# A carry scan over chunk ends: nine narrow steps in place of seven wide ones

## The reference, cut to what matters

```python
x = x + layernorm(attn(layernorm(x)))       # x: 8 x 1024 x 512
x = x + layernorm(ffn(layernorm(x)))

def attn(x):
    s = sigmoid(silu(x @ s_w1.T + s_b1) @ s_w2.T + s_b2)
    u = (x @ B_w.T + B_b) * s                # 8 x 1024 x 128
    h[t] = h[t - 1] @ A.T + u[t]             # the recurrence over 1024 tokens, h[-1] = 0
    y = h @ C_w.T + C_b + x @ D_w.T + D_b
    return y * sigmoid(x @ g_w.T + g_b)

def ffn(x):
    out_shared = relu(x @ Ws1) ** 2 @ Ws2
    # and a sum over routed experts, weighted by trunc(softmax of the two best)
    return out_shared + out_routed
```

## Time and profile before

| | us |
|---|---|
| median of 3 runs | 800.49 (800.29 to 800.89) |
| profiled execution, its own time | 800.6 |
| span of that execution (first to last instruction) | 798.6 |
| PE busy | 783.3 (98%) |
| PEld busy (beside PE) | 648.0 (81%) |
| DVE busy | 605.9 (76%) |
| POOL busy | 456.4 (57%) |
| ACT busy | 344.4 (43%) |

### The profile page before, as it was taken

The page is one execution under the profiler, slowest core; times in us unless marked ns, Lnnn a source line. Parts: engine busy times, 40 slices in busy tenths (PEclk is TensorE's granted clock), DMA queues, the critical chain, the costliest instruction groups (busy, mean ns, idle before and its releaser), DMA issues. The chain is left out here.

```text
span 798.6 us, 10778 instructions
## 1 busy us (share of the span) xinstructions
PE 783.3 (98%) x3628; PEld 648.0 (81%) x3628; DVE 605.9 (76%) x1404; ACT 344.4 (43%) x554; POOL 456.4 (57%) x553
## 2 busy tenths in 40 slices
PE   7999999999999999999999999999999999999996
PEld 6878888888888888888888888888888888888875
DVE  7868896598956897678975889649896589734895
ACT  4535354344434554245443535435443444432353
POOL 1253658548465576466674665845757557644445
PEclk9999999999999999999999999999999999999999
DMA  8534434454355425552345533454425442232222
GB/s 269 207 107 158 137 94 138 160 184 134 87 177 174 161 89 158 183 187 80 95 143 185 185 101 96 147 185 168 149 80 182 150 143 80 78 133 87 65 113 106
DMA packets 40767, 110.90 MB, mean 139 GB/s; under 512 B 7044, under 2 KB 24836, under 8 KB 32903
## 3 DMA queue, kind: packets, MB, share of 16 engines
q1 hardware_dynamic: 40278, 110.00, 41.4%
q10 hardware_dynamic: 432, 0.20, 0.1%
HBM read 60.84 MB, written 33.61 MB: 118 GB/s over the span
## 5 line engine op out<-in xcount | busy, mean ns | idle before, releaser
L499 PE MATMUL TM<-gw_hi,xT_hi 128*128 128x512 f32 x256 | 107.3, 419 | 0.0
L1982 POOL TENSOR_TENSOR xres<-work,xres 128x512 f32<-128x512 f32 x56 | 75.1, 1341 | 52.8 <-DVE work L1332 52.8
L501 PE MATMUL TM<-gw_hi,xT_lo 128*128 128x512 f32 x256 | 100.6, 393 | 0.0
L501 PE MATMUL TM<-dw_hi,xT_lo 128*128 128x512 f32 x256 | 100.2, 391 | 0.0
L500 PE MATMUL TM<-gw_lo,xT_hi 128*128 128x512 f32 x256 | 100.0, 391 | 0.0
L499 PE MATMUL TM<-dw_hi,xT_hi 128*128 128x512 f32 x256 | 99.9, 390 | 0.0
L500 PE MATMUL TM<-dw_lo,xT_hi 128*128 128x512 f32 x256 | 99.6, 389 | 0.0
L996 ACT ACTIVATE work<-TM,nmz,rsz 128x512 f32<-128x512 f32 x62 | 48.2, 777 | 106.7 <-POOL nmz L1952 106.7
L1942 POOL TENSOR_TENSOR rsv<-rsv,negh 128x1 f32<-128x1 f32 x64 | 47.1, 736 | 82.3 <-DVE rsv L1328 82.2
L1997 POOL TENSOR_TENSOR x2T_lo<-work,x2T_hi 128x512 fp32r<-128x512 f32 x60 | 78.5, 1319 | 2.0 <-ACT x2T_hi L926 1.9
L1990 POOL TENSOR_TENSOR work<-work,xres 128x512 f32<-128x512 f32 x60 | 76.7, 1295 | 1.3 <-ACT work L996 1.3
(11 more groups left out here) (189 smaller groups left out, 2063.1 us busy)
## 6 DMA issues: line engine op xcount, KB each, us to landing
xres<-in_x SPq DMA_DIRECT2D x16, 1024.0 KB, 5.9
x_scratch<-xres SPq DMA_DIRECT2D x16, 1024.0 KB, 4.7
xin<-in_x SPq DMA_DIRECT2D x15, 1024.0 KB, 5.3
work<-x2q SPq DMA_DIRECT2D x120, 128.0 KB, 2.7
out<-work SPq DMA_DIRECT2D x30, 512.0 KB, 3.2
xin<-in_x_t SPq DMA_DIRECT2D x14, 1024.0 KB, 6.2
rows_in<-ln_scratch SPq DMA_DIRECT2D x14, 512.0 KB, 4.7
xin<-in_x SPq DMA_DIRECT2D x2, 512.0 KB, 5.0
```

The costliest lines, as they stand in the source:

```text
L499: eng.matmul(ps, lhs[0], rhs[0], start=first, stop=False)
L501: return eng.matmul(ps, lhs[1], rhs[0], start=False, stop=last)
L1982: eng.tensor_tensor(xres[:, j, :], work[:, j, :], xres[:, j, :], ALU.add).then_inc(S["x1_ok"], 1)
```

## The change

Nine steps carry over the chunk ends in place of seven. The odd columns are added to the even ones (pairs), every second pair to the next (pairs of pairs), five doubling steps run over every fourth column, and two steps go down again, to the columns 6, 10, .. and then to the odd ones. They read and write `carry` at strides of 2 and 4 columns. The slices sum to 64 + 32 + 31 + 30 + 28 + 24 + 16 + 31 + 63 = 319 columns. The inner steps become 10 to 16, so a scan has 17 steps. The lists of PE, ACT, DVE and POOL in the tails are written anew.

```diff
--- before.py
+++ after.py
...
@@ -218,6 +218,10 @@
                 POWERS.append((at[3 * k], plain, at[2 * k]))
             k, plain = 2 * k, twice
 
+        CARRY_STEPS = [(slice(1, 128, 2), slice(2, 129, 2), L), (slice(2, 127, 4), slice(4, 129, 4), 2 * L)]
+        CARRY_STEPS += [(slice(4, 129 - 4 * s, 4), slice(4 + 4 * s, 129, 4), 4 * L * s) for s in (1, 2, 4, 8, 16)]
+        CARRY_STEPS += [(slice(4, 125, 4), slice(6, 127, 4), 2 * L), (slice(2, 127, 2), slice(3, 128, 2), L)]
+
         def power_of(i):
             return (SC, *TR)[i % 3][:, 0:P]
 
@@ -534,11 +538,12 @@
                     for j in range(L - 1):
                         m = eng.matmul(SC[:, 0:P], apt[:, idx[L - 1 - j], :], u[:, j, :],
                                        start=(j == 0), stop=(j == L - 2))
-                elif i <= 7:
-                    s = 2 ** (i - 1)
-                    m = eng.matmul(SC[:, s:P], apt[:, idx[L * s], :], carry[:, 1:1 + P - s], start=True, stop=True)
+                elif i <= 9:
+                    src, dst, k = CARRY_STEPS[i - 1]
+                    n = (dst.stop - dst.start - 1) // dst.step + 1
+                    m = eng.matmul(SC[:, 0:n], apt[:, idx[k], :], carry[:, src], start=True, stop=True)
                 else:
-                    j = i - 8
+                    j = i - 10
                     prev = carry[:, 0:P] if j == 0 else u[:, j - 1, :]
                     m = eng.matmul(SC[:, 0:P], apt[:, 0, :], prev, start=True, stop=True)
                 m.then_inc(S["scan_done"], 1)
@@ -690,34 +695,32 @@
 
             def first_tail(b, rep):
                 a = (b, rep)
-                G(*a, 0, {0: 0, 2: 1})
-                scan_step(*a, 2)
-                G(*a, 1, {0: 3, 1: 4, 2: 5})
-                scan_step(*a, 6)
-                G(*a, 2, {0: 7, 1: 8, 2: 9})
-                scan_step(*a, 10)
+                G(*a, 0, {0: 0, 1: 1, 2: 2})
+                scan_step(*a, 3)
+                G(*a, 1, {0: 4, 1: 5, 2: 6})
+                scan_step(*a, 7)
+                G(*a, 2, {0: 8, 1: 9, 2: 10})
                 scan_step(*a, 11)
-                G(*a, 3, {1: 12})
-                scan_step(*a, 13)
-                scan_step(*a, 14)
+                G(*a, 3, {0: 12, 1: 13, 2: 14})
+                scan_step(*a, 15)
+                scan_step(*a, 16)
 
             def tail(b, rep):
                 a = (b, rep)
                 G(*a, 0, {0: 0, 1: 1, 2: 2})
-                W1f(*a, 1, 0)
-                scan_step(*a, 3)
-                W1f(*a, 1, 1, {0: 4})
-                G(*a, 1, {0: 5, 1: 6})
-                scan_step(*a, 7)
-                G(*a, 2, {1: 8, 2: 9})
-                scan_step(*a, 10)
+                W1f(*a, 1, 0, {1: 3})
+                scan_step(*a, 4)
+                W1f(*a, 1, 1, {0: 5, 2: 6})
+                G(*a, 1, {0: 7, 1: 8})
+                scan_step(*a, 9)
+                G(*a, 2, {0: 10, 1: 11, 2: 12})
                 W2(*a, 4)
-                scan_step(*a, 11)
+                scan_step(*a, 13)
                 W2(*a, 5)
-                scan_step(*a, 12)
-                G(*a, 3, {2: 13})
+                scan_step(*a, 14)
+                G(*a, 3, {1: 15})
                 W2(*a, 6)
-                scan_step(*a, 14)
+                scan_step(*a, 16)
                 W2(*a, 7)
 
             def body(b, rep):
@@ -757,14 +760,15 @@
                 scan_step(*a, 4)
                 W1f(*a, 1, 1, {0: 5, 1: 6})
                 scan_step(*a, 7)
-                G(*a, 1, {0: 8, 1: 9})
-                G(*a, 2, {1: 10, 2: 11})
+                G(*a, 1, {0: 8, 1: 9, 2: 10})
+                G(*a, 2, {0: 11, 1: 12})
+                scan_step(*a, 13)
                 W2(*a, 4)
                 W2(*a, 5)
-                G(*a, 3, {0: 12, 1: 13})
+                G(*a, 3, {0: 14, 1: 15})
                 W2(*a, 6)
+                scan_step(*a, 16)
                 W2(*a, 7)
-                scan_step(*a, 14)
 
             def last_body(b, rep):
                 a = (b, rep)
@@ -903,7 +907,7 @@
             def hs(b, rep, j):
 
                 if j < L - 1:
-                    eng.wait_ge(S["scan_ok"], body_at("scan_ok", b, 8 + j))
+                    eng.wait_ge(S["scan_ok"], body_at("scan_ok", b, 10 + j))
                 if j >= 2:
                     eng.wait_ge(S["y_done"], body_at("y_done", b, j - 2))
                 src = u[:, j, :] if j < L - 1 else carry[:, 1:P + 1]
@@ -999,9 +1003,9 @@
             def first_tail(b, rep):
                 a = (b, rep)
                 gate(*a, 0)
-                hs(*a, 0)
                 gate(*a, 1)
                 gate(*a, 2)
+                hs(*a, 0)
                 gate(*a, 3)
                 hs(*a, 1)
 
@@ -1009,13 +1013,13 @@
                 a = (b, rep)
                 hidden(*a, 1, 0)
                 hidden(*a, 1, 1)
-                hs(*a, 0)
                 gate(*a, 0)
                 gate(*a, 1)
+                hs(*a, 0)
+                hs(*a, 1)
                 gate(*a, 2)
                 zn(*a, 4)
                 zn(*a, 5)
-                hs(*a, 1)
                 gate(*a, 3)
                 zn(*a, 6)
                 zn(*a, 7)
@@ -1075,17 +1079,17 @@
 
             def last_tail(b, rep):
                 a = (b, rep)
+                gate(*a, 0)
                 hidden(*a, 1, 0)
-                gate(*a, 0)
+                gate(*a, 1)
                 hidden(*a, 1, 1)
-                gate(*a, 1)
+                hs(*a, 0)
                 gate(*a, 2)
-                hs(*a, 0)
                 zn(*a, 4)
                 zn(*a, 5)
                 gate(*a, 3)
+                hs(*a, 1)
                 zn(*a, 6)
-                hs(*a, 1)
                 zn(*a, 7)
 
             def last_body(b, rep):
@@ -1294,11 +1298,12 @@
                     if rep > 0:
                         eng.wait_ge(S["hs_hi_ok"], body_at("hs_hi_ok", b - 1, L - 1))
                     r = eng.tensor_tensor(carry[:, 1:P + 1], SC[:, 0:P], u[:, L - 1, :], ALU.add)
-                elif i <= 7:
-                    s = 2 ** (i - 1)
-                    r = eng.tensor_tensor(carry[:, 1 + s:P + 1], SC[:, s:P], carry[:, 1 + s:P + 1], ALU.add)
+                elif i <= 9:
+                    _, dst, _ = CARRY_STEPS[i - 1]
+                    n = (dst.stop - dst.start - 1) // dst.step + 1
+                    r = eng.tensor_tensor(carry[:, dst], SC[:, 0:n], carry[:, dst], ALU.add)
                 else:
-                    j = i - 8
+                    j = i - 10
                     r = eng.tensor_tensor(u[:, j, :], SC[:, 0:P], u[:, j, :], ALU.add)
                 r.then_inc(S["scan_ok"], 1)
 
@@ -1474,90 +1479,94 @@
                 scan_add(*a, 0)
                 l1_bn(b + 1, 0)
                 scan_add(*a, 1)
+                l1_bn(b + 1, 1)
                 scan_add(*a, 2)
-                l1_bn(b + 1, 1)
+                l1_bn(b + 1, 2)
                 scan_add(*a, 3)
-                l1_bn(b + 1, 2)
+                l1_ag(b + 1, 0)
                 scan_add(*a, 4)
-                l1_ag(b + 1, 0)
                 l1_ag(b + 1, 1)
-                l1_bn(b + 1, 3)
                 scan_add(*a, 5)
                 scan_add(*a, 6)
+                l1_ag(b + 1, 2)
                 scan_add(*a, 7)
+                l1_bn(b + 1, 3)
                 scan_add(*a, 8)
                 scan_add(*a, 9)
-                hs_low(*a, 0)
-                l1_ag(b + 1, 2)
+                l1_bn(b + 1, 4)
                 l1_ag(b + 1, 3)
+                l1_bn(b + 1, 5)
                 l1_ep(b + 1, 0)
                 scan_add(*a, 10)
-                l1_bn(b + 1, 4)
+                scan_add(*a, 11)
+                scan_add(*a, 12)
                 l1_ag(b + 1, 4)
-                scan_add(*a, 11)
-                l1_bn(b + 1, 5)
+                l1_ag(b + 1, 5)
                 l1_bn(b + 1, 6)
-                l1_ag(b + 1, 5)
+                scan_add(*a, 13)
+                l1_ag(b + 1, 6)
                 l1_bn(b + 1, 7)
-                l1_ag(b + 1, 6)
-                scan_add(*a, 12)
-                scan_add(*a, 13)
+                scan_add(*a, 14)
+                scan_add(*a, 15)
+                scan_add(*a, 16)
+                hs_low(*a, 0)
+                hs_low(*a, 1)
                 l1_ag(b + 1, 7)
                 l1_ep(b + 1, 1)
-                hs_low(*a, 1)
-                scan_add(*a, 14)
 
             def tail(b, rep):
                 a = (b, rep)
                 l1_bn(b + 1, 0)
+                l1_bn(b + 1, 1)
                 scan_add(*a, 0)
-                l1_bn(b + 1, 1)
+                l1_bn(b + 1, 2)
                 scan_add(*a, 1)
+                l1_bn(b + 1, 3)
+                l1_ag(b + 1, 0)
                 scan_add(*a, 2)
-                l1_bn(b + 1, 2)
-                l1_ag(b + 1, 0)
+                scan_add(*a, 3)
                 l1_ag(b + 1, 1)
-                l1_bn(b + 1, 3)
                 l1_bn(b + 1, 4)
-                l1_bn(b + 1, 5)
```

(64 more changed lines are left out.)

## The result

| | before | after |
|---|---|---|
| median of 6 runs each, us | 800.39 (800.18 to 800.89) | 803.76 (803.37 to 804.23) |
| profiled execution, its own time | 800.6 | 803.77 |
| its span | 798.6 | 801.7 |

The ratio is 1.0043, 95% interval [1.0032, 1.0053]: slower by 3.4 us. The forecast was 804.0.

A forecast was written before the change was run, and what follows sets the result against it. The prediction took TensorE's queue as the bound, without waits from the second pass to the last carry stage. Two extra steps a pass, 3.7 us, less 0.2 in the first pass gave 3.5, so 804.0 us, range 802.8 to 806.4.

The forecast's parts named there:

- main term: TensorE's queue: two more fp32 steps in each of 8 passes, 0.46 us a pass, 3.7 us in all.
- (1) Columns: Carry steps on TensorE: 450 columns fewer a pass save nothing; taken as 0.
- The bound of 0.37 us a pass: Carry steps on TensorE: most that 450 fewer columns could save, at 0.41 ns a column and two records.
- (2) Two steps: TensorE, every pass: two steps more cost 2 x 0.232 = 0.46 us, with no idle time to take them.
- (3) Strides: Carry tile, strides 2 and 4: cost 0; VectorE's 32-column adds take 170 ns if free, 292 if not.
- (4) The longer chain: Six ordinary tails: additions still arrive in time, 0 (0 to 0.3 us each); tightest at steps 10 to 12, about 0.1 spare.
- (5) Last pass: Last pass's new order: addition of step 12 ends 0.2 us before step 13 is due; cost 0, at most 0.5.
- (6) First pass: First pass: one back-to-back pair saved (0.65), a wait of about 0.4 at step 11; net -0.2, between -0.65 and +0.2.
- (7) Moved items: Work moved on GpSimd, VectorE and SP's queue comes about 0.4 us later but is absorbed by VectorE's idle time; 0.
- columns: Rival: TensorE's steps cost their columns alone, so the change is faster, 797.3 us; chance 0.04, in part 0.07 with others.
- late adds: Rival: VectorE's carry additions come late, ordinary tails stall 0.2 to 0.3 us each plus about 0.1; 806 us; chance 0.18.
- strides: Rival: VectorE's 32-column adds at stride 4 take 0.45 us, stalling close pairs 0.1 to 0.2; 805 to 806 us; chance 0.05.

The follow-up runs named there:

- e3: Changed kernel with the matmuls of its two steps down (8 and 9) left out, their waits, signals and additions kept; 800.30 us, ratio 1.0001.
- e1: Kernel before with its seven carry steps cut to 64, 32, 31, 30, 28, 24 and 16 contiguous columns; 800.43 us, ratio 1.0001.
- e7: Kernel before with 13 fewer, wider scan matmuls a pass in place of 21, ordinary and last carry-stage lists set anew; 802.09 us, ratio 1.0021.
- e6: Kernel before with 13 fewer, wider scan matmuls a pass in place of 21, steps near their old places in the lists; 803.54 us, ratio 1.0037.
- e4: Kernel before plus two one-record fp32r matmuls of 16 columns a pass, one weight load each, into an unread bank; 803.47 us, ratio 1.0041.
- e2: Kernel before plus two fp32 matmuls of 16 columns in each pass's body, into a bank nobody reads; 804.09 us, ratio 1.0047.
- e5: Changed kernel with l1_ep 0 and l1_bn 5 moved behind addition 10 in VectorE's first-pass list; 804.01 us, ratio 1.0044.
- e8: Changed kernel with the e5 list edit, and the first pass's G 3 written into its own PSUM bank; 803.46 us, ratio 1.0038.

## Why the prediction was right, point by point

Its main term is the cause: the kernel after and e3 differ by the two matmuls alone, and by 3.5 us. That the whole sum came within 0.3 us is in part luck. Over whole passes of these two runs the steps make 3.9 us, where 3.7 was forecast. The -0.2 beside them was put on the first tail, but that is 0.14 longer in e3 than before; it is the six ordinary tails (-0.28 in all), where a gain was called excluded, and the stretch behind the last tail (-0.20) that gave something back.

**(1) Columns: 0, right, for a reason that was half right.** The price around a step is flat from 127 down to 16 columns (0.227 to 0.239 us), as two rows at 126 and 64 had said, and e1 shows it alone. The 0.41 ns a column, taken from the records' lengths, was wrong: above 128 columns a record streams 0.83 to 0.85 ns a column (e7: half of 1.7). The bound of 0.37 us a pass would have been 0.75 by that. It did no harm here because none of the columns is paid. e6 and e7, which priced an fp32 step of 512 columns like two ordinary matmuls (0.45 ns a column and record), erred by the same factor of about two. A modelled end is no duration; the price of a width is read from starts around steps on both sides of it.

What the flat price is was only argued. By the Trainium skill, "TensorE: Matmul & The Clock Gate", section LDWEIGHTS (loading the stationary operand), a load takes about P / 1.2 ns, for 128 columns an estimate of 107 ns, so 213 ns for a step's two loads. The measured 0.227 to 0.239 us around two loads and 0.121 around the one of e4 agree with it to some 15 ns a load. Over whole bodies it is 0.245 and 0.16, and the one load of e4 lies 53 ns above the estimate. e4 halves the records along with the loads, and no run here changes the size of a load, so that the loads are the floor stays argued.

**(2) Two steps: 0.46 us a pass, right.** It is 0.44 to 0.47 in the six ordinary tails, 0.49 to 0.50 in e2, and gone in e3. Between e3 and the kernel after, alike but for the two matmuls, the ordinary tails differ by 0.49 to 0.51: a step moves what follows by 0.245 us, and the window of two matmuls behind it misses the last 0.01. So the new order itself gave back some 0.04 a tail, which the forecast took as excluded. Where it comes from was not tried.

**(3) Strides: 0, right, the sizes off.** The adds were put at 170 ns for 32 columns if the stride was free, 292 if it was not; measured are 192 without and 219 with stride 4. The line was drawn too steep, 1.3 ns a column, because its row of 64 columns, 211 ns, is a mean of two kinds: six of the eight additions begin 81 to 87 ns before the end of VectorE's instruction ahead of them and are recorded as 205 to 209 ns, the two others as 225 and 226. Without so much overlap the additions do lie on a line (before and e1): 292, 259, 225, 192 and 176 ns at 127, 96, 64, 32 and 16 columns, 1.05 ns a column on top of some 158. Stride 4 makes this steeper: 11 ns more at 16 columns, 20 at 24, 24 at 31 and 27 at 32, some 0.7 to 0.9 ns a column. Both ends lie under the 292 ns that the chain had the earlier trace rows, so nothing is late. By the Trainium skill, "SBUF — State Buffer", section Door 1: The DMA port swizzle, each access that crosses to a new 16-byte line pays a penalty. In the trace an addition at stride 4 in fp32, each value in a new line, takes 11 to 27 ns more and one at stride 2, two values to a line, 1 ns more, which agrees.

**(4) The longer chain: 0 for ordinary tails, right.** No wait from 60 to 760 us. The tightest place, steps 10 to 12, is at 142.95, 143.87 and 144.79; VectorE in between, after (timeline: start, us; idle before, releaser):

```profile
143.37 0.29 DVE L1307 TENSOR_TENSOR u<-SC,u 128x128 f32<-128x128 f32 x1
144.04 0.29 DVE L1313 TENSOR_TENSOR hs_lo<-u,hs_hi 128x128 fp32r<-128x128 f32 x1 [0.38 <-ACT hs_hi L914]
144.29 0.29 DVE L1307 TENSOR_TENSOR u<-SC,u 128x128 f32<-128x128 f32 x1
```

Counted from step 10: the addition at 0.42 (0.42 forecast), hs_low at 1.09 (1.10), the addition of step 11 at 1.34 (1.34 to 1.38), step 12 due and started at 1.84. That addition ends at 1.63, where the forecast had 1.67, and with the 0.06 from an addition's end to the next step 0.15 us are left, where the forecast had about 0.1.

**(5) Last pass: 0 beside the two steps, nearly.** It grew by 0.54; e3, without the two matmuls, still shows 0.07. That is the list's, within the 0.5 allowed. Behind the last tail, where everything was to shift with TensorE, the kernel after is 0.19 shorter and e3 0.20; why was not tried.

**(6) First pass: the step that failed, by 0.3 us.** The forecast was -0.2 beside the two steps, within -0.65 and +0.2; measured is 0.57 - 0.46 = +0.1. The saving of one back-to-back pair (0.65) and the wait at step 11 are there. The timeline of TensorE and VectorE in the first pass, after, against the earlier trace rows:

```profile
53.26 0.40 PE L505 MATMUL TM<-gw_hi,xT_lo 128*128 128x512 f32 x1
53.83 0.49 PE L548 MATMUL SC<-u,apt 128*128 128x128 f32 x2 [0.17 <-DVE u L1307]
54.34 0.50 PE L503 MATMUL TM<-gw_hi,xT_hi 128*128 128x512 f32 x1
```

```profile
52.17 0.68 DVE L1224 BATCH_NORM_STATS2 st<-xin 128x6 f32<-128x512 f32 x1
52.77 0.16 DVE L1228 BATCH_NORM_AGGREGATE mv<-st 128x2 f32<-128x6 f32 x1
52.85 0.66 DVE L1224 BATCH_NORM_STATS2 st<-xin 128x6 f32<-128x512 f32 x1
53.43 0.15 DVE L1233 TENSOR_SCALAR ve<-mv 128x4 f32<-128x4 f32 x1
53.49 0.28 DVE L1307 TENSOR_TENSOR u<-SC,u 128x128 f32<-128x128 f32 x1
```

The four statistics hold addition 10 until 53.49, and step 11 starts 0.57 behind the ordinary matmul instead of 0.23: 0.34 lost there. Then G 3 starts 0.51 behind step 11. Of this 0.14 is usual. Another 0.10 followed the step that waited in the kernel before (0.24 in the earlier trace rows); the forecast counted that for the pair that it saved and not for this wait. The other 0.27 is for G 2's bank, which ScalarE's gate 2 reads until 54.29:

```profile
53.69 0.60 ACT L905 ACTIVATE work<-TM 128x512 f32<-128x512 f32 x1 [3.06 <-PE TM L505]
```

With these, -0.65 + 0.34 + 0.10 + 0.27 = +0.06, near the measured +0.1. In the kernel before, steps 10 and 11 stood back to back between G 2 and G 3, and their wait covered the gate: it ended at 54.46 there, and G 3 started at 54.67. The prediction counted that pair's wait as wholly saved, and did not ask what else it had been covering. e5 and e8 show both: without the statistics in the way nothing is gained, with a bank of its own as well the tail is 17.92, which is 18.09 + 0.46 - 0.65 = 17.90, the best first pass of the forecast. The bank without the change in the list was not run.

**(7) Moved items: 0, right.** No wait in the bodies, and e3 with all of them moved takes the time of before.

Of the rivals, columns fell with e1, late adds with the empty list of waits and with e3, strides with the adds of 219 ns at 32 columns, where that rival needed 450.

## What to carry to other kernels

Price a small matmul by the starts of ordinary matmuls on either side of it, at two widths, before counting columns, and check the price on the length of a whole stage, which here showed 0.01 to 0.04 us more a matmul than its neighbours did. In this kernel only the number of steps counted up to 128 columns, and only the columns from 256 on: fewer columns saved nothing in the narrow steps, and fewer but wider steps next to nothing in the tails. And where a wait goes away on an in-order engine, look for what it covered: the next buffer that the same engine needs may have come free only just in time.

## What the runs showed that was not expected

An fp32 step of this kernel has a price of 0.227 to 0.239 us around it at any width from 16 to 128 columns, 0.44 to 0.45 at 256 and 0.87 at 512. The line through the last two meets the floor near 130 columns (an estimate, as no width between 128 and 256 was run), about where the kernel already worked. An addition of VectorE does not shrink in proportion to its columns (292 ns at 127 columns, 225 at 64, 192 at 32, 176 at 16), a stride of 4 fp32 values costs it 0.7 to 0.9 ns a column where a stride of 2 costs 1 ns in all at 64 columns, and the record of an addition that begins some 80 ns before the end of the instruction ahead is some 20 ns shorter.
